# Three norms' reciprocal roots, taken for both batches of a pair at once, and new orders on five queues

## The reference

```python
def L0(queries, keys, values, attention_mask, ...):        # 16 heads of 16
    q, k, v = relu(queries @ Wq + bq), relu(keys @ Wk + bk), relu(values @ Wv + bv)
    scores = einsum('bhqd,bhkd->bhqk', q_, k_) / sqrt(dh)
    scores = where(m, scores, 1e-09)                       # m: attention_mask of the query
    x = softmax(scores) @ v_ + queries
    return (x - mu) * rsqrt(var + EPS) * gamma + beta      # a layer norm: the first root

def mamba2_block(x, ...):                                  # 8 heads of 64, state of 128
    zxbcdt = rms(x, norm_w) @ in_proj_w                    # the second root; 256 -> 1288 columns
    z, xBC, dt = split(zxbcdt); dt = softplus(dt + dt_bias)
    xBC = silu(conv_b + causal depthwise conv, 4 taps)
    xh, Bm, Cm = split(xBC)
    h_t = h_(t-1) * exp(dt * A) + dt * xh_t * B_t; y_t = h_t . C_t
    u = rms((y + D_skip * xh) * silu(z), gnorm_w)
    return x + u @ out_proj_w

def cross_attention(x, enc, ...):                          # 8 heads of 32
    xn = (x - mu) * rsqrt(v + EPS) * ln_w + ln_b           # the third root
    return x + softmax(mask((xn @ Wq) (enc @ Wk)^T / sqrt(dh))) @ (enc @ Wv) @ Wo

x = L0(x, ctx, ctx, mask_BxS2_ik0, ...)
return cross_attention(mamba2_block(x, ...), ctx, mask_1xS2_bf0, ...)
```

## Time and profile before

| | us |
|---|---|
| median of 3 runs | 1337.02 (1336.65 to 1338.48) |
| span of the profiled execution | 1337.2 |
| busy: TensorE, its weight loads | 1291.6 (97%), 1148.0 (86%) |
| busy: VectorE | 1208.1 (90%) |
| busy: ScalarE | 1130.8 (85%) |
| busy: GpSimd | 928.7 (69%) |

### The profile page before, as it was taken

How to read it: one execution, slowest core, us unless ns; L and a number is a source line. 1 busy time by engine, 2 the same in 40 slices (tenths; PEclk the granted TensorE clock), 3 DMA queues, 4 the chain that set the end, 5 groups by cost and what they waited for, 6 DMA issues and landing times.

```text
span 1337.2 us, 43414 instructions
## 1 busy us (share of the span) xinstructions
PE 1291.6 (97%) x15624; PEld 1148.0 (86%) x15624; DVE 1208.1 (90%) x3056; ACT 1130.8 (85%) x3407; POOL 928.7 (69%) x1200
## 2 busy tenths in 40 slices
PE   5879999999999999999999999999999999999987
PEld 4668889988888998889998889989888898888875
DVE  6789999999999999999999999999999989999982
ACT  5658989888889988888988888998888898888875
POOL 3366777777767777777777776777777777766774
PEclk9889999999999999999999999999999999999999
DMA  6102221212221112222121222211222221111110
GB/s 203 40 34 72 69 77 38 70 56 69 77 77 62 52 49 69 77 77 77 38 66 60 69 77 77 61 53 50 69 77 77 71 71 34 62 56 57 49 57 25
DMA packets 41283, 87.00 MB, mean 65 GB/s; under 512 B 5744, under 2 KB 10992, under 8 KB 41072
## 3 DMA queue, kind: packets, MB, share of 16 engines
...
...
q10 hardware_dynamic: 864, 0.42, 0.1%
...
## 4 chain that ended last, share of the span: by engine, by line
PE 87%; DVE 4%; ACT 4%; issue 2%; DMA 1%; POOL 1%; SPq 1%; ACTq 0%; DVEq 0%
PE bank L319 26%; PE bank L422 10%; PE bank L550 6%; PE bank L412 5%; PE bank L379 5%; PE bank L533 5%; PE bank L436 4%; PE bank L564 4%; PE bank L669 4%; PE bank L360 3%; PE bank L604 3%; PE bank L625 2%; PE bank L654 2%; PE bank L470 2%; PE bank L416 1%
## 5 line engine op out<-in xcount | busy, mean ns | idle before, releaser
L951 DVE SCALAR_TENSOR_TENSOR ACC<-bank,cw,ACC 128x250 f32<-128x250 f32 (+2 forms) x576 | 264.1, 462 | 5.9 <-ACT ACC L1535 3.3
L319 PE MATMUL bank<-xnT,wnl 128*128 128x256 f32 x640 | 201.6, 315 | 3.3 <-DVE xnL L883 2.3
L1622 ACT ACTIVATE PC<-bank,stc 128x128 f32<-128x128 f32 x512 | 182.5, 389 | 7.7 <-DVE stc L1068 4.3
L319 PE MATMUL bank<-xnL,wnh 128*128 128x256 f32 x640 | 180.3, 282 | 0.0
L319 PE MATMUL bank<-xnT,wnh 128*128 128x256 f32 x640 | 179.8, 281 | 0.0
L800 DVE TENSOR_REDUCE sta<-bank 128x4 f32<-128x512 f32 x256 | 163.7, 673 | 7.8 <-PE bank L379 7.5
L977 DVE TENSOR_TENSOR_SCAN L<-DB,id 128x1024 f32<-128x1024 f32 x64 | 146.8, 2293 | 0.8 <-DMA DB<-dec_scratch 0.8
L319 PEld LDWEIGHTS bank<-xnT,wnl 128*128 128x128 f32 x640 | 121.9, 190 | 26.0 <-issue 17.6
L1437 ACT ACTIVATE PTA<-bank 128x512 f32<-128x512 f32 x256 | 133.3, 628 | 9.0 <-PE bank L416 5.3
L1916 POOL TENSOR_TENSOR PC<-PC,stc 128x512 f32<-128x512 f32 x128 | 132.1, 1042 | 11.3 <-DVE stc L1075 11.3
L319 PEld LDWEIGHTS bank<-xnL,wnh 128*128 128x128 f32 x640 | 122.4, 191 | 0.0
...
## 6 DMA issues: line engine op xcount, KB each, us to landing
...
```

Of the source, the lines that this page charges most:

```text
L319: mm = e.matmul(t[:, c0:c0 + T], wt[:, k, m:m + 128], x[:, k, :], start=(n == 0), stop=(n == 5))
L951: e.scalar_tensor_tensor(out=w, in0=t[:, 0:T].rearrange("p (b t) -> p b t", b=NB)[:, :, 0:125 + k], scalar=cw[:, c, k:k + 1], in1=w, op0=A ...
L1622: op = e.activation(PC[n % 4][:, p, :], t[:, p * 128:(p + 1) * 128], ACT.Exp, bias=stc[g % 4][:, 4 * i + p:4 * i + p + 1], accum_out=stc[g ...
```

## The change

**One root for two batches.** The rings `sta`, `stb` and `stn` of four tiles become rings `STA`, `STB` and `STN` of two, each with a dimension for the batch; the old names are views of them. `rs`, `nr` and `hr` on GpSimd and `hm` on VectorE lose their argument b: one call does both batches of a pair on 128x2, waits until both are there, and raises its semaphore by 2.

```diff
-        sta = ring("sta", 4, [128, 48])
-        stb = ring("stb", 4, [128, 16])
-        stn = ring("stn", 4, [128, 1])
+        STA = ring("STA", 2, [128, NB, 48])
+        sta = [STA[n // NB][:, n % NB, :] for n in range(4)]
+        STB = ring("STB", 2, [128, NB, 16])
+        stb = [STB[n // NB][:, n % NB, :] for n in range(4)]
+        STN = ring("STN", 2, [128, NB, 1])
+        stn = [STN[n // NB][:, n % NB, :] for n in range(4)]
...
-            def rs(g, b):
-                if ok(g):
-                    ns = 2 * g + b
-                    w = sta[ns % 4][:, 33:34]
-                    e.wait_ge(s_bg, ns + 1)
+            def rs(g):
+                if ok(g):
+                    w = STA[g % 2][:, :, 33:34]
+                    e.wait_ge(s_bg, 2 * g + 2)
                     e.tensor_scalar(w, w, EPS, None, ALU.add).then_inc(s_be, 1)
-                    e.wait_ge(s_be, ns + 1)
-                    e.tensor_tensor(w, w, mhalf[:, :], ALU.pow).then_inc(s_rs, 1)
...
+                    e.wait_ge(s_be, g + 1)
+                    e.tensor_tensor(w, w, mhalf[:, :].unsqueeze(1).to_broadcast([128, NB, 1]), ALU.pow).then_inc(s_rs, 2)
...
-            def hr(g, b):
-                if ok(g):
-                    ns = 2 * g + b
-                    w = stb[ns % 4][:, 3:4]
-                    e.wait_ge(s_hg, ns + 1)
+            def hr(g):
+                if ok(g):
+                    w = STB[g % 2][:, :, 3:4]
+                    e.wait_ge(s_hg, 2 * g + 2)
                     e.tensor_scalar(w, w, EPS, None, ALU.add).then_inc(s_hb, 1)
-                    e.wait_ge(s_hb, ns + 1)
-                    e.tensor_tensor(w, w, mhalf[:, :], ALU.pow).then_inc(s_hr, 1)
+                    e.wait_ge(s_hb, g + 1)
+                    e.tensor_tensor(w, w, mhalf[:, :].unsqueeze(1).to_broadcast([128, NB, 1]), ALU.pow).then_inc(s_hr, 2)
...
-            def hm(g, b):
-                if ok(g):
-                    ns = 2 * g + b
-                    w = stb[ns % 4]
-                    e.wait_ge(s_hr, ns + 1)
-                    e.scalar_tensor_tensor(out=w[:, 10:11], in0=w[:, 2:3], scalar=-1.0, in1=w[:, 3:4],
-                                           op0=ALU.mult, op1=ALU.mult).then_inc(s_hm, 1)
+            def hm(g):
+                if ok(g):
+                    w = STB[g % 2]
+                    e.wait_ge(s_hr, 2 * g + 2)
+                    e.scalar_tensor_tensor(out=w[:, :, 10:11], in0=w[:, :, 2:3], scalar=-1.0, in1=w[:, :, 3:4],
+                                           op0=ALU.mult, op1=ALU.mult).then_inc(s_hm, 2)
```

```diff
-    (("k", 1, 1), 3), (("ot", 0, 2), 5), (("z", 1, 3), 2), (("sT", 4, 2), 1), (("sT", 5, 2), 5), (("sT", 6, 2), 6),
...
+    (("cp", 5, 3), 7), (("z", 1, 3), 2), (("av", 0, 2), 3), (("tn", 1, 2), 1), (("k", 1, 1), 6), (("tC", 0, 5), 0),
...
-            sT(0, 0); k(1, 1); av(0, 0); av(0, 1); av(0, 2); av(0, 3); tn(0, 1); ot(0, 0); q(2, 0); sT(0, 1); q(2, 1)
...
+            v(1, 0); sT(0, 0); av(0, 0); av(0, 1); tn(0, 1); av(0, 2); av(0, 3); k(1, 1); sT(0, 1); ot(0, 0)
```

1034 lines of the change are left out of this document (505 added, 529 removed), and 20 rows, old and new, of the table USES.

## The result

The kernel after takes **1369.23 us** (median of 4 runs, 1366.28 to 1369.97) and the kernel before 1337.75 (4 runs, 1336.65 to 1338.5): a ratio of 1.023, 95% interval 1.0214 to 1.0245. It is 2.3% slower. The forecast of 1331.9 was wrong in its sign, and the time lies outside its range. The profiled execution's span is 1367.6 us, 30.4 more than before.

A forecast was written before the change was run, and what follows sets the result against it. TensorE, busy 97%, was taken as the bound, with its round of 39.5 us, the ramp and the drain to look at: 1337.2 - 2.8 (round) - 2.5 (ramp) + 0 (drain) = 1331.9 us, range 1322 to 1343.

The forecast's parts named there:

- The round's own work: TensorE's loop: fewer switches of array shape, net -2.8 us, between -4.2 and +3.0; round 39.4 us against 39.54.
- The edge in question: TensorE, `sT` to `sA`: taken as free since both use 32 rows; priced like a switch, the term becomes +3.0 us.
- The ramp: Start of the kernel: -2.5 us (+1 to -6), 1.2 from an earlier `ot(0,1)` chain and 1.3 on VectorE.
- Behind one maximum and one other: VectorE, 60 to 80 us: `lg(0,0)` has three fewer maxima ahead, 2.0 us; with products gone, 1.3 us taken.
- GpSimd's roots: GpSimd: 96 additions and 96 powers fewer, 75 us of its busy time, but 0 us in the middle.
- `hm`: VectorE's merged product, issued 32 times instead of 64: 17 us of VectorE saved, 0 us in the middle.
- Rival 1: Slower: TensorE's `sA` waits for `kk1` behind `hm` and merged `hr`, 0.4 us in 28 rounds; 1343 us; chance 0.19.
- The drain: End of the kernel: TensorE's list is the same from `o(31,0)` on; 0 us, from -2 to +2.

The follow-up runs named there:

- stale: The kernel after, but each read of DB takes the previous pair's decays, so the wait for the write is already met (output wrong); 1358.62 us.
- stale_pe: stale with `tn(1,1)` and `sT(1,1)` moved ahead of `sA(2,0)` in TensorE's start; 1354.0 us.
- ramp_split: The kernel after with `sA(2,0)` behind `tn(1,1)` and `sT(1,1)`, and pair 0's `rs` issued per batch again, `x2(0,0)` following at once; 1357.92 us.
- split: The kernel after with its orders, but the three roots and `hm` done once per batch again; 1363.83 us.
- stale_bd: stale with the single transpose `bd` moved behind `sT` in TensorE's loop; 1393.77 us.

## Why the prediction was wrong, point by point

**The step that failed: no term for the decays.** The round was priced on TensorE alone, with one rival on VectorE, `hm` and GpSimd. VectorE's new order was read for `kk1` and not for the distance from `dk` to the scan. The page's row (0.8 us for 64 scans) looked like nothing at stake, but it says only that the slack was not used up, and not how much there was. It was 1.4 to 3.4 us, the 8.4 us of distance less the 5.0 to 7.0 that the data took. The new order took 1.3 of them on VectorE, the reads took another 1.1 in the mean, and the scan then lost its place ahead of `nC`. Nothing in the prediction priced a scan and a GpSimd instruction side by side, though it had seen `hm` held that way. stale gave 10.6 us back. By size the term of the ramp, below, missed by more.

The round of the forecast's rows, 39.54 us long, was itself not the usual one of 39.48.

**The round's own work: forecast -0.10, measured +0.16 us.** The edge in question was judged rightly. From the last instruction of `sT` to the first of `sA` it takes 0.30 us, against 0.40 to transposes or a projection. This agrees with the rule that the forecast took from the Trainium skill's TensorEngine Tiling (Key Properties), that it is a change of the mode that drains: no price of leaving the shape is seen here. In an undisturbed round 17 intervals between different shapes (4.24 us) became 16 (3.86 us), 0.38 less. What was missed is the rest, which grew by 0.54 us with the same instructions. The edges themselves have more than one price too: `o` to `bd` to `sT` takes 0.11 + 0.20 where `o` to `sT` took 0.18, and `wp` to `y` takes 0.31 where the projection `dp` to `y` took 0.19. By which rule those differ isn't shown. The term is 0.26 us x some 26 rounds, 6 to 7 us off.

**The ramp: forecast -2.5, measured +12.** `sT(0,1)` came at 29.07 (28 said), `sA(1,0)` at 33.28 (31.9) and `ot(0,1)` at 37.83 (35 to 37), since `xo(0,0)` itself was 1.35 us later, as the whole trace was from its first `sT` on. The text said it would be wrong if `ot(0,1)` came earlier and `nt(0,0)` did not, and this is so: `wouth`'s copies took 1.70 us between the squares as forecast, and `x2(0,0)`, behind `rs(0)` for both batches, came 7.4 us later (1.35 of them `xo`'s). ScalarE, after:

```profile
42.70 0.42 ACT L1455 ACTIVATE junk<-X 128x256 uint8<-128x256 f32 x1 [5.01 <-DVE X L864]
43.24 1.70 ACT L1453 ACTIVATE wouth<-PTC,pc 128x256 fp32r<-128x256 f32 x4
```

The large mistake was in the next sentence. "Behind one maximum and one other" counted instructions ahead of `lg(0,0)`. The "other" was `rc(1,1)`, which waits for TensorE, and TensorE's own list had put a call that waits for VectorE ahead of it: `lg(0,0)` came 1.5 us later and not 2.0 earlier. A queue's place was priced by what is ahead in it, and not by what that waits for; and the first `y`, on which the term was built, no longer waited for `lg(0,0)` at all. The call is worth 4.6 us by stale and stale_pe. The merged `rs` costs 2 to 3 (ramp_split, split), and the rest of the 14.8 us by which the term was off, above all the 6 us between 100 and 150, stays open.

**GpSimd's roots.** A power on 128x2 took 0.70 to 0.74 us (0.6 taken), an addition 0.22 to 0.35. Groups of after (out<-in count | busy, mean ns | idle before):

```profile
L1849 POOL TENSOR_TENSOR DX<-XC,pc 128x512 f32<-128x512 f32 x64 | 118.4, 1850 | 3.7 <-DVE Y L1006 2.4 <-DVE XC L959 1.3
...
L1832 POOL TENSOR_TENSOR STA<-STA,mhalf 128x2 f32<-128x2 f32 x32 | 23.5, 735 | 4.7
...
L1042 DVE SCALAR_TENSOR_TENSOR STB<-STB 128x2 f32<-128x2 f32 x32 | 6.0, 186 | 1.3 <-POOL STB L1896 1.3
```

0 us in the middle held. GpSimd's busy time of 855 us did not (944.8): in the new order 27 of the 64 `dx` start beside a scan and take 2.95 us each, the others 1.05. In the mean that is 1850 ns, where before took

```profile
L1862 POOL TENSOR_TENSOR DX<-XC,pc 128x512 f32<-128x512 f32 x64 | 68.8, 1075 | 0.5 <-DVE XC L964 0.4
```

which is 50 us more by itself. **`hm`** counted 0 and was 0: 186 ns each, since a GpSimd instruction runs beside it in 3 of 32 cases (519 ns in the mean, against 152), and in 61 of 64 before (561, against 129). VectorE is busy for 1199.7 us (1190 said).

**Rival 1** had the size of TensorE's slack (0.3 us) and the kind of loss right, a round of 39.9 or more from a late block on VectorE, and its time of 1343 was the nearest, still 26 us short. Its place was wrong: TensorE never waited for `kk1` in the middle.

**The drain: 0 (±2), measured +4.4.** The last scan before it, `scan(28,0)`, waits 1.41 us for its decays in a round of 44.28 (0.52 and 43.12 in stale), and `tC(31,0)` waits for `fin` in a bank that the new list gives to both (1180 to 1368 us):

```profile
PE bank L423 <- DVE X L1075: 2.0, 1, 2.0
```

The rest of it is open. In stale_pe 5.6 us of the end stay, 3.0 of the start at 250 us, and 3.3 of the middle, by the alignment; that is the 11.9 by which its span (1349.1) is over before's. Open too is why the write is slow for some pairs: in after's order the pairs 18 to 24 had the quick one in nearly every version (stale_bd has one of 1.88), and in before's only where `dk` was moved.
